# Expert stage: high weights of the first layer meet both halves of a tile in one matmul of 256 columns

## The reference, cut to what matters

```
scores = einsum('bne,ex->bnx', x, Wg) + bg
topk_vals, topk_idx = top_k(scores, 2);  gates = softmax(topk_vals)
h = einsum('bne,xeh->bnxh', x, W1) + b1          # 256 -> 384, 8 experts
h = gelu(h, approximate=False)
expert_out = einsum('bnxh,xhe->bnxe', h, W2) + b2  # 384 -> 256
out = sum over the two chosen experts of gate * expert_out
```

## Time and profile before

| | us |
|---|---|
| median of three executions | 478.45 (476.68 to 479.4) |
| span of the profiled execution | 494.5 |
| PE busy in it | 375.3 (76%) |
| DVE busy | 310.4 (63%) |
| POOL busy | 201.3 (41%) |
| ACT busy | 184.4 (37%) |

### The profile page before, as it was taken

The page is one execution under the profiler, slowest core; times in us unless marked ns, Lnnn a source line. Parts: engine busy times, 40 slices in busy tenths (PEclk is TensorE's granted clock), DMA queues, the critical chain, the costliest instruction groups (busy, mean ns, idle before and its releaser), DMA issues.

```text
span 494.5 us, 8809 instructions
## 1 busy us (share of the span) xinstructions
PE 375.3 (76%) x2955; PEld 254.4 (51%) x2955; DVE 310.4 (63%) x652; ACT 184.4 (37%) x360; POOL 201.3 (41%) x152
## 2 busy tenths in 40 slices
PE   0999869999899998897966791145987888888523
PEld 0646545566466652543455471035765667667422
DVE  3656363389933896689988678953444454445365
ACT  1343634344342440241414646105433444335223
POOL 3203443133331320065545456551655655555422
PEclk9999999999999998899866896557999998989856
DMA  8900000000000700002270224211222222222195
GB/s 243 373 2 2 0 1 1 1 0 2 0 1 2 212 2 2 2 0 64 65 201 13 64 65 148 85 54 33 76 76 87 76 76 76 77 80 72 66 303 207
DMA packets 27050, 36.00 MB, mean 73 GB/s; under 512 B 7328, under 2 KB 22560, under 8 KB 26880
## 3 DMA queue, kind: packets, MB, share of 16 engines
q1 hardware_dynamic: 20880, 22.98, 14.6%
q0 software_dynamic: 3952, 10.37, 7.2%
q10 hardware_dynamic: 2176, 2.10, 1.3%
HBM read 26.13 MB, written 9.31 MB: 72 GB/s over the span
## 4 chain that ended last, share of the span: by engine, by line
PE 42%; DVE 29%; issue 11%; ACT 5%; another core or an unknown queue 4%; DMA 4%; POOL 1%; SPq 1%; ACTq 0%; DVEq 0%
PE ps L1338 17%; PE ps L1583 8%; PE ps L1569 8%; PE ps L1441 3%; DVE sm L898 3%; DVE u_h L908 2%; DVE t L1217 2%; DMA cols<-in_L_conv_bv_dram 2%; DVE tiles L1164 2%; PE ps L1557 1%; ACT late L774 1%; DMA l<-expert_rows_dram 1%; DVE work L971 1%; PE ps L1493 1%
## 5 line engine op out<-in xcount | busy, mean ns | idle before, releaser
L1569 PE MATMUL ps<-late,l 128*128 128x128 f16 x702 | 97.0, 230 | 16.1 <-issue 9.7
L1583 PE MATMUL ps<-l,late 128*128 x351 | 87.1, 283 | 7.8 <-issue 6.4
L1569 PEld LDWEIGHTS ps<-late,l 128*128 x702 | 63.9, 103 | 30.2 <-issue 22.8
L479 POOL TENSOR_TENSOR tiles<-tiles 128x1024 f16<-128x1024 f32 x16 | 34.5, 2158 | 94.3 <-ACT tiles L704 94.3
L559 POOL DMA_INDIRECT expert_rows_dram<-late,idx x39 | 38.8, 994 | 53.7 <-DVE late L1207 48.6
L774 ACT ACTIVATE late<-ps,b_sb 128x128 f32<-128x128 f32 x117 | 34.4, 365 | 67.9 <-remote 47.3
L1441 PE MATMUL ps<-u_h,tiles 128*128 128x256 f16 x256 | 44.5, 272 | 9.0 <-DVE u_l L909 9.0
L1207 DVE TENSOR_TENSOR late<-ps,qk 128x256 f32<-128x256 f32 x39 | 16.6, 424 | 52.0 <-remote 36.3
L1338 PE MATMUL ps<-l 128*128 128x512 f16 x192 | 44.2, 380 | 0.1
L555 POOL DMA_INDIRECT late<-token_rows_dram,idx x39 | 37.9, 972 | 14.8 <-issue 11.3
L1583 PEld LDWEIGHTS ps<-l,late 128*128 128x128 f16 x351 | 34.6, 99 | 15.2 <-issue 8.3
(11 more groups left out here) (304 smaller groups left out, 780.6 us busy)
## 6 DMA issues: line engine op xcount, KB each, us to landing
prep<-in_L_ffn_W_dram SPq DMA_DIRECT2D x16, 384.0 KB, 3.3
l<-expert_rows_dram SPq DMA_DIRECT2D x16, 256.0 KB, 5.8
l<-in_x_dram SPq DMA_DIRECT2D x4, 512.0 KB, 8.6
token_rows_dram<-val SPq DMA_DIRECT2D x2, 1024.0 KB, 4.6
l<-in_inv_f_dram SPq DMA_DIRECT2D x1, 1536.0 KB, 6.2
out_dram<-l SPq DMA_DIRECT2D x3, 512.0 KB, 2.8
qk<-in_L_ffn_b_dram SPq DMA_DIRECT2D x8, 128.0 KB, 3.8
fwd_hi_sb<-in_fwd_hi_dram SPq DMA_DIRECT2D x1, 768.0 KB, 12.2
```

The costliest lines, as they stand in the source:

```text
L479: PL.tensor_tensor(Pt[1][:, n % 2, :], prob[:, n % 2, :], Pt[0][:, n % 2, :], ALU.subtract).then_inc(p_low, 1)
L1569: last = PE.matmul(psh[s % 2][:, m * P:(m + 1) * P], experts[:, bass.ds(e, 1), o:o + P].rearrange("p a c -> p (a c)"), xT[:, s % 2, (r * C ...
L1583: last = PE.matmul(psy[s % 2], hh[l][:, s % 3, m * P:(m + 1) * P], experts[:, bass.ds(e, 1), o:o + C].rearrange("p a c -> p (a c)"), start ...
```

## The change

The matmuls of `hidden` are paired. For each chunk m and input chunk k, the high weights are loaded once and meet the high and the low half of the tile in one matmul of 256 columns, whose output falls in two adjacent pieces of 128 columns; the low weights meet the high half in a matmul of 128 columns that adds to the second piece. The two pieces are then summed: ScalarE copies the second piece with the bias added into `hsum` (three instructions of 128 columns), VectorE adds the first piece (one instruction over 384 columns, `hidden_sum`), and ScalarE applies Gelu to the sum (one instruction over 384 columns). `hidden` now waits for the sum of tile s - 2 instead of its Gelu. PSUM for the hidden values grows from two banks to four (2, 3, 6, 7). ACT does `hidden_biased(i)` and then `hidden_values(i - 1)`; DVE does `hidden_sum(i - 1)` between `take_gathered(i)` and `hidden_low(i - 2)`. PE interleaves twelve hidden matmuls with the nine of `results`.

```diff
-        psh = [ps[:, 2, 0:HC * P], ps[:, 3, 0:HC * P]]
+        psh = [ps[:, 2:4, :].rearrange("p a n -> p (a n)"), ps[:, 6:8, :].rearrange("p a n -> p (a n)")]
+        hsum = view(late, 21, [2, HC * P], F32)
...
-            for s in range(TILES):
+            def hidden_biased(s):
+
                 e = act.value_load(where[0:1, s:s + 1], min_val=0, max_val=E - 1)
                 act.wait_ge(hid_full, s + 1)
+                for m in range(HC):
+                    last = ACTV(hsum[:, s % 2, m * P:(m + 1) * P], psh[s % 2][:, (2 * m + 1) * P:(2 * m + 2) * P], ACT.Identity,
+                                bias=b1_sb[:, bass.ds(e, 1), m])
+                last.then_inc(hid_biased, 1)
+
+            def hidden_values(s):
+
+                act.wait_ge(hid_summed, s + 1)
                 if s >= 3:
                     act.wait_ge(hid_low, s - 2)
-                for m in range(HC):
-                    last = ACTV(hf[:, s % 3, m * P:(m + 1) * P], psh[s % 2][:, m * P:(m + 1) * P], ACT.Gelu,
-                                bias=b1_sb[:, bass.ds(e, 1), m])
-                last.then_inc(gelu_done, 1)
+                ACTV(hf[:, s % 3, :], hsum[:, s % 2, :], ACT.Gelu).then_inc(gelu_done, 1)
                 act.wait_ge(gelu_done, s + 1)
                 if s >= 3:
                     act.wait_ge(y_full, s - 2)
                 ACTV(hh[0][:, s % 3, :], hf[:, s % 3, :], ACT.Identity).then_inc(hid_high, 1)
+
+            for i in range(TILES + 1):
+                if i < TILES:
+                    hidden_biased(i)
+                if i >= 1:
+                    hidden_values(i - 1)
...
+            def hidden_sum(s):
+
+                dve.wait_ge(hid_biased, s + 1)
+                wide = hsum[:, s % 2, :].rearrange("p (m t) -> p m t", m=HC)
+                upper = psh[s % 2][:, 0:HC * 2 * P].rearrange("p (m r t) -> p m r t", m=HC, r=2)[:, :, 0, :]
+                V.tensor_tensor(wide, upper, wide, ALU.add).then_inc(hid_summed, 1)
...
                     take_gathered(i)
+                if 0 <= i - 1 < TILES:
+                    hidden_sum(i - 1)
                 if 0 <= i - 2 < TILES:
                     hidden_low(i - 2)
...
                 pe.wait_ge(x_taken, s + 1)
                 if s >= 2:
-                    pe.wait_ge(gelu_done, s - 1)
+                    pe.wait_ge(hid_summed, s - 1)
                 e = at_expert[s % 16]
+                both = xT[:, s % 2, :].rearrange("p (r k t) -> p k r t", r=2, k=CC)
                 for m in range(HC):
-                    for n, (l, r, k) in enumerate([(l, r, k) for k in range(CC) for l, r in ((0, 0), (0, 1), (1, 0))]):
-                        o = l * CC * H + k * H + m * P
-                        last = PE.matmul(psh[s % 2][:, m * P:(m + 1) * P], experts[:, bass.ds(e, 1), o:o + P].rearrange("p a c -> p (a c)"),
-                                         xT[:, s % 2, (r * CC + k) * P:(r * CC + k + 1) * P], start=(n == 0), stop=(n == 3 * CC - 1))
-                        if (m, n) == (HC - 1, 3 * CC - 1):
-                            last.then_inc(hid_full, 1)
-                        yield
+                    for k in range(CC):
+                        for l in range(2):
+                            o = l * CC * H + k * H + m * P
+                            at_m = 2 * m * P + l * P
+                            last = PE.matmul(psh[s % 2][:, at_m:2 * (m + 1) * P], experts[:, bass.ds(e, 1), o:o + P].rearrange("p a c -> p (a c)"),
+                                             both[:, k, 0:2 - l, :], start=(k == 0 and l == 0), stop=(k == CC - 1), skip_group_check=True)
+                            if (m, k, l) == (HC - 1, CC - 1, 1):
+                                last.then_inc(hid_full, 1)
+                            yield
...
                 for n in range(3 * HC):
                     next(first, None)
                     next(second, None)
-                    next(first, None)
+                    if n % HC == HC - 1:
+                        next(first, None)
```

More of the change, by code:

```diff
@@ L366, in conv_attn_moe_kernel @@
         scattered = [sem(f"scattered{k}") for k in range(4)]
+        hid_summed, hid_biased = sem("hid_summed"), sem("hid_biased")
         x_turned, x_taken, hid_full, gelu_done, hid_high, hid_low, y_full, y_taken = (
```

## The result

The changed kernel takes 504.87 us (median of four executions, 497.97 to 507.38), the kernel before 478.91 us (four executions, one more than the 478.45 us rest on): ratio 1.049, 95% interval 1.038 to 1.060. A repetition in a later session gave 501.94 against 475.69 us, ratio 1.059 (1.045 to 1.073). Forecast were 497.5 us, 19.1 us of loss, and a range of 483 to 504. The way was right. The median lies 0.9 us above the range, and by the ratio the time is 1.049 x 478.45 = 501.9 us, inside it.

The account below looks back on a forecast made before the run. PE's sequencer was taken to bound at 2.79 us per tile, then a loop through ACT and DVE at 3.29: 36 x (3.29 - 2.79) = 18.0 us plus 1.1 at the end, 478.45 + 19.1 = 497.5 us, range 483 to 504.

Parts of the forecast that it names:

- PE's bound before: Expert stage: PE's sequencer, with 18 register operations per tile, sets the pace at 2.79 us, the array close behind.
- the price per operation: PE's sequencer: one register operation with what follows it costs about 0.125 us, 18 of them 2.25 us per tile.
- rival 2: Fewer weight loads and matmuls pay on PE, 0.09 us each: loop 3.08 us per tile, 490 us; chance 8%.
- The new loop: Last hidden matmul through ACT, DVE and the cast back to PE: 6.57 us per two tiles, 3.29 per tile, becomes the bound.
- PE's round inside the loop: First to last hidden matmul of a round: 2.47 us less 0.12 us saved, 2.35 us.
- the tile of the kernel before: Expert stage before the change: 2.79 us per undisturbed tile, subtracted from 3.29 us for the loss per tile.
- the pauses: PE waits of 1.03 to 1.16 us in the expert stage, 19 us in all, mostly in the profiled execution alone.
- The end of the stage: Last hidden matmul to last low half grows from 1.82 to 2.97 us, delaying results, scatter and read-back: 1.1 us.
- How PE waits: First hidden matmul released by VectorE's cast in most tiles, some 0.5 us idle each; transposes 3.2 to 3.4 us apart.
- rival 1: The pauses are in the timed runs too, so the loop replaces time already lost: 3 us more, 481.5 us; chance 12%.
- Rival 3: Faster: the loop doesn't bind and PE's period falls: 474 us, at most down to 470.5 us; chance 5%.
- Rival 4: PE, standing still more, falls to the lower clock for stretches: about 502 us or more; chance 5%.

Follow-up runs that it names:

- e4: Changed kernel with the paired matmuls kept, the sum removed and Gelu straight from PSUM as before the change; computation incomplete: 475.88 us, ratio 1.003 to the kernel before.
- e7: e4 with the low weights replaced by the high ones, so two matmuls share an address, 12 register operations per tile instead of 18; computation incomplete: 472.08 us.
- e1: The kernel before, run again unchanged: 477.77 us, ratio 0.992.
- e3: Changed kernel with VectorE's order made cast of i + 1, result of i - 4, sum of i - 1, low half of i - 2: 478.6 us, ratio 1.002 to the kernel before.
- e8: Kernel before with pairing moved to the second layer: low and high weights as one 512-column operand from one address, VectorE adding the pieces: 469.16 us, ratio 0.977.
- e6: Changed kernel with ScalarE doing a tile's Gelu and high half right after its own biased copies: 489.24 us, ratio 1.026 to the kernel before.

## Why the prediction was right, and its size off

**PE's bound before: right, the price per operation too simple.** 18 register operations per tile, not the matmuls, set the pace (e4, e7). In the trace of e1, 538 of the 701 starts of such an operation come 0.124 or 0.125 us after the one before, the prediction's 0.125. 18 of them are 2.25 us and four transposes 0.23; an ordinary tile there takes 2.74 us (the median of the last 33 periods), and what fills the rest no run takes apart. Nor does each one less save 0.125 us: six less made it 0.52 us (e7). The 2.20 us left are 0.055 us per 128 columns, about the 0.057 at which the transposes start, so the columns seem to bind there; their 2.28 us in the prediction were a little high.

The runs bear out nothing of rival 2: six pairs of weight load and matmul fewer gave 0.02 us a tile (e4). The Trainium skill, page "TensorE: Matmul & The Clock Gate", section "Back-to-back issue gap", has 81 ns for such a pair with 128 columns, by which the prediction estimated 0.32 us for the six. e4 alone might hide a saving behind the register operations; e7 does not, since its 25 pairs in an undisturbed tile take 2.20 us, and by the figures that the prediction used they would take 10 x 81 + 15 x 109 ns = 2.45 us, an estimate.

**The new loop: right, link by link.** The timeline of ACT, DVE and PE in the changed kernel (start us, length us), over one turn of the loop; its first line is the last hidden matmul of the round before:

```profile
396.51 0.22 PE L1596 MATMUL ps<-late,l 128*128 128x128 f16 x1
...
396.87 0.88 ACT L775 ACTIVATE late<-ps,b_sb 128x128 f32<-128x128 f32 x3 [2.04 <-PE ps L1596]
397.64 0.53 ACT L784 ACTIVATE late<-late 128x384 f32<-128x384 f32 x1
397.79 0.56 DVE L1216 TENSOR_TENSOR late<-ps,late 128x384 f32<-128x384 f32 x1 [1.07 <-ACT late L775]
...
398.20 0.52 ACT L788 ACTIVATE late<-late 128x384 f16<-128x384 f32 x1
398.76 0.56 DVE L1222 TENSOR_TENSOR late<-late 128x384 f16<-128x384 f32 x1 [0.41 <-ACT late L788]
...
399.59 0.42 DVE L1229 TENSOR_TENSOR late<-ps,qk 128x256 f32<-128x256 f32 x1 [0.27 <-PE ps L1610]
...
399.93 0.68 DVE L1209 CAST late<-ps 128x512 f16<-128x512 f32 x1
...
400.75 0.28 PE L1596 MATMUL ps<-late,l 128*128 128x256 f16 x1 [1.07 <-DVE late L1209]
...
403.29 0.22 PE L1596 MATMUL ps<-late,l 128*128 128x128 f16 x1
...
403.65 0.88 ACT L775 ACTIVATE late<-ps,b_sb 128x128 f32<-128x128 f32 x3 [2.20 <-PE ps L1596]
```

From the copies: Gelu after 0.77 us (taken 0.77), high half 0.56 later (0.56), low half 0.56 (0.55), result 0.83 (0.83), cast 0.34 (0.34), its end and PE's first matmul at 400.75, 0.82 (0.82). From the last hidden matmul to the next first one that is 4.24 us, where 4.22 was forecast, and 4.24 us is also the median of the 17 such ways from the sixth round on in this trace. The Gelu takes 0.53 us and the sum 0.56 us, as taken from the nearest rows. The sum ends before the low half begins, so it is hidden, as said.

**The terms that were mis-sized: PE's round inside the loop, and the tile of the kernel before.** The prediction took 2.47 - 0.12 = 2.35 us for the first to the last hidden matmul. It is 400.75 to 403.29, 2.54 us, in this turn, and 2.46 us in the median of these 17 rounds. The 0.12 us that shorter runs of matmuls behind one register operation were to save aren't there (e4: 0.02). The next first matmul after a wait comes at 407.54:

```profile
407.54 0.28 PE L1596 MATMUL ps<-late,l 128*128 128x256 f16 x1 [1.04 <-DVE late L1209]
```

407.54 - 400.75 = 6.79 us for two tiles. This turn is a slow one of its kind: the median of the 16 turns from the sixth round on is 6.69 us, 3.35 per tile, against 6.57 and 3.29 forecast. And 2.79 us for a tile before was read from the execution with the pauses; the repetition has 2.74. So the loss per tile is 3.35 - 2.74 = 0.61 us where 0.50 was forecast, half of the difference from either end, and 36 x 0.61 = 22 us instead of 18.0. Over all tiles it comes to the same: the first five periods take 13.0 us against 10.5 in the repetition of the kernel before, the other 33 on average 3.42 against 2.84, together the 21.8 us measured. (The averages lie above the ordinary tile because every eighth tile is 0.6 to 1.4 us longer in both kernels: there PE reads up to eight expert numbers.)

The end of the stage cost 1.5 us, not 1.1: last hidden matmul to last result is 468.24 to 474.43 in the changed kernel, 6.2 us, and was 461.00 to 465.72, 4.7 us, before. It is less sure than the rest, for the repetition of the changed kernel has 7.3 us. Stage and end are 23.3 us together, which fits the ratio 1.049 (23.5 us of 478.9). Both mis-sized terms pushed the forecast the same way, to too small a loss; no errors cancelled.

**How PE waits: wrong in its form.** I expected about 0.5 us of idle in most tiles. The one-line view of line 1596 has 21 waits of 1 us:

```profile
  issue: 32.1, 39
  DVE late L1209: 20.4, 21
```

The loop closes over two rounds, and only one of the two chains, of the even or of the odd rounds, is late: after a wait PE does two rounds on end (transposes at 399.29, 403.37, 406.11, 410.00), since the cast for the second was made under the first. So neighbouring transposes are by turns 3.6 to 4.6 and 2.7 to 3.1 us apart, not 3.2 to 3.4 each. The sum over two tiles is the same, so it did no harm to the forecast.

**The pauses: right to leave them out** (e1, rival 1 wrong). Rival 3 asked for a way from last hidden matmul to next first one under 2.99 us; e3 takes the cast out of it and shows PE's own pace again, 105.1 us, with nothing gained over 104.3. Rival 4: the granted clock stayed at its upper level over the stage, though PE stands still; the 0.98 below is short of 1 only by the first microseconds of the stretch. Nor does the clock explain the difference between the kernels: in the traces of e1 and of the changed kernel it rises 5.1 and 5.5 us after the stage's first transposes and stays up to its last. Busy time by stretch, PE, PEld, DVE, ACT, POOL, clock, DMA share, GB/s:

```profile
335.00:462.00 127.00, 103.80 (x906) 74.88 (x906) 75.11 (x141) 66.51 (x181) 70.03 (x69) 0.98 0.25 74
```

## What to carry to other kernels

Where operand addresses are computed at run time, count a stage's distinct addresses per tile before its matmuls; here merging two matmuls that already shared an address saved nothing (e4), merging two that didn't saved 8 us of 104 (e8). When a tile gets one more hop between engines, write down each engine's order and follow one full turn of the loop: 2.2 us of VectorE work per 2.8 us tile looked safe, and cost 22 us by its place alone; moving the cast and the result ahead of it gave them back (e3). And compare stage by stage, with a second profiled execution, before believing a trace with waits for nothing.

## What the runs showed of the hardware that was not expected

In these kernels PE's sequencer started one register operation per distinct run-time address, and most of them 0.124 or 0.125 us after the one before (e1: 538 of 701). VectorE's register read started under the instruction two ahead of the one that uses it where no wait stood between: 0.60 instead of 0.83 us from low half to result in e6. And one profiled execution held some 22 us of pauses in the expert stage (126.9 against 104.3 us) that no other profiled execution of these kernels had; where they come from stays open.
